# Linear attention on one core: scores from a block-diagonal q, or head by head in row groups of 32

## What is computed

```python
xn = layernorm(x)                       # 2048 x 512
q, k, v, u = split(xn @ W_qkvu.T, 4);  q, k = silu(q), silu(k)      # 16 heads of 32
# for each block of tokens and each head, with a state kv (32 x 32):
o = (q * q_decay) @ kv + ((q @ k.T) * diag_decay) @ v
kv = block_decay * kv + (k * k_decay).T @ v
branch1 = (u * (o * rsqrt(mean(o * o) + eps))) @ W_out.T
idx = sort(top_k(xn @ w_router, 256));  branch2 = xn, with attention and MLP on xn[idx]
out = x + branch1 + branch2
```

## Time and profile before

| | us |
|---|---|
| median of 3 runs | 670.95 |
| lowest, highest run | 670.15, 677.82 |
| span of the profiled execution (first to last instruction) | 664.6 |
| median less span | 6.3 |
| TensorE matmuls busy in the span | 563.0 (85%) |
| VectorE, ScalarE, GpSimd busy | 406.3 (61%), 332.8 (50%), 256.9 (39%) |

### The profile page before, as it was taken

The page is one execution under the profiler, slowest core; times in us unless marked ns, Lnnn a source line. Parts: engine busy times, 40 slices in busy tenths (PEclk is TensorE's granted clock), DMA queues, the critical chain, the costliest instruction groups (busy, mean ns, idle before and its releaser), DMA issues.

```text
span 664.6 us, 10529 instructions
## 1 busy us (share of the span) xinstructions
PE 563.0 (85%) x3946; PEld 496.2 (75%) x3946; DVE 406.3 (61%) x777; ACT 332.8 (50%) x574; POOL 256.9 (39%) x149
## 2 busy tenths in 40 slices
PE   2897999999999999999989665594678768789993
PEld 2787888898898888988868554484577757589992
DVE  5648546644655555555677877687988996513231
ACT  4786544454463455544778780234545544545430
POOL 3435334223332332332221443545430522247771
PEclk9897999999999999999998987796789897989998
DMA  9300012101001110001000414232311123115432
GB/s 289 138 18 31 2 33 33 33 2 33 33 2 33 34 33 0 18 17 50 30 17 1 143 34 125 99 103 87 126 64 64 64 72 119 65 64 175 154 117 32
DMA packets 24067, 42.93 MB, mean 65 GB/s; under 512 B 4112, under 2 KB 4112, under 8 KB 23888
## 3 DMA queue, kind: packets, MB, share of 16 engines
q1 hardware_dynamic: 23472, 40.93, 19.0%
q0 software_dynamic: 544, 1.31, 1.1%
...
## 4 chain that ended last, share of the span: by engine, by line
PE 58%; issue 13%; DVE 13%; ACT 9%; POOL 3%; DMA 2%; SPq 1%; ACTq 0%; DVEq 0%; POOLq 0%
PE bank L1116 17%; PE bank L1072 9%; PE bank L1074 8%; PE bank L1073 8%; PE bank L1109 6%; PE bank L1161 3%; ACT marks L398 2%; DVE rope L849 2%; PE bank L1198 2%; DVE staged L852 2%; DMA XX<-in_x 2%; PE bank L1220 2%; DVE rope L847 2%; PE bank L1142 1%; ACT whi L420 1%
## 5 line engine op out<-in xcount | busy, mean ns | idle before, releaser
L1022 POOL TENSOR_TENSOR wlo<-raw,whi 128x2048 fp32r<-128x2048 f32 x24 | 112.0, 4668 | 121.1 <-ACT whi L420 121.1
L1116 PE MATMUL bank<-xTh,Wh 128*128 128x256 f32 x384 | 120.1, 313 | 8.2 <-DVE Wl L630 4.9
L1116 PE MATMUL bank<-xTl,Wh 128*128 128x256 f32 x384 | 110.3, 287 | 0.0
L1116 PE MATMUL bank<-xTh,Wl 128*128 128x256 f32 x384 | 110.2, 287 | 0.0
L1116 PEld LDWEIGHTS bank<-xTh,Wh 128*128 128x128 f32 x384 | 75.2, 196 | 20.4 <-issue 16.7
L683 DVE TENSOR_TENSOR QBl<-QT,QBh 32x256 fp32r<-32x256 f32 x128 | 73.9, 577 | 13.7 <-ACT QBh L391 12.4
L1072 PE MATMUL bank<-HTh,whi 128*128 128x256 f32 x224 | 66.5, 297 | 14.4 <-DVE staged L840 9.7
L1116 PEld LDWEIGHTS bank<-xTl,Wh 128*128 128x128 f32 x384 | 75.3, 196 | 0.2
L1116 PEld LDWEIGHTS bank<-xTh,Wl 128*128 128x128 f32 x384 | 75.0, 195 | 0.0
L1073 PE MATMUL bank<-HTl,whi 128*128 128x256 f32 x224 | 66.4, 296 | 0.0
L1074 PE MATMUL bank<-HTh,wlo 128*128 128x256 f32 x224 | 66.2, 296 | 0.0
...
## 6 DMA issues: line engine op xcount, KB each, us to landing
...
```

Source lines behind the costliest of these rows:

```text
L1022: Q.tensor_tensor(wlo[b % 3][:], raw[b % 2][:], whi[b % 3][:].bitcast(f32), ALU.subtract)\
L1116: ins = T.matmul(bank[:, half * GROUP:(half + 1) * GROUP], w[:, k, cols], xt[:, g % 2, k, :], start=m % steps == 0, stop=m % steps == step ...
```

## The change

The block-diagonal operand goes. q is kept as it is, in `qh` and `ql` (rows, 4 tiles, 128 tokens), each written by one instruction of 512 elements per partition. `score(N)` does all 16 heads at once: for each tile j and each of the three products, four matmuls, one a head, each contracting only its 32 rows (a row group of the array) over 128 columns, and each into a bank of its own (0, 1, 6, 7). `by_row` puts `A` and `DEC` into the order of the banks. The attention output, the sum of squares and the output projection now share bank 4; turned keys, transposes and keys-by-values share bank 5; the ranking's small products use bank 2. The order within a chunk becomes: score, tile 0, rms(N-1), keys turned, tile 1, output projection (N-1), transposes, tile 2, `attend` (state part, then all 16 heads in a row), new keys-by-values, tile 3. On VectorE the mask comes first in a chunk, and the state product last. On GpSimd `q_decayed(N)` stands in slot N rather than in the slot before it. Two memsets of the old operand fall away.

```diff
-        QBh, QBl = (sb(n, [P, 2, 4, P], f32r, ca) for n in ("QBh", "QBl"))
+        qh, ql = (sb(n, [P, NK, P], f32r, ca) for n in ("qh", "ql"))
...
         B = [ctx.enter_context(nc.psum_tensor(f"bank{i}", [P, 512], f32)) for i in range(8)]
 
-        def score_bank(N, half, b):
-
-            return B[2 + b] if half and N >= N_TILES - CH else B[b]
+        score_banks = [B[0], B[1], B[6], B[7]]
+        out_bank, turn_bank, pick_bank = B[4], B[5], B[2]
+
+        def by_row(h):
+
+            return NK * (h % 4) + h // 4
 
...
-            def q_high(N, half):
-
-                act.wait_ge(proj_sb, NPROJ * (N // CH) + 4), act.wait_ge(bm_ok, 1)
-                act.wait_ge(s_ps, 2 * N + half), act.wait_ge(q_lo, 2 * N + half)
+            def q_high(N):
+
+                act.wait_ge(proj_sb, NPROJ * (N // CH) + 4)
+                act.wait_ge(s_ps, N), act.wait_ge(q_lo, N)
                 cols = slice(N % CH * P, (N % CH + 1) * P)
-                for r in range(4):
-                    rows = slice(DH * r, DH * r + DH)
-                    ins = S.activation(QBh[rows, :, r, :], QT[rows, N // CH % 2, 2 * half:2 * half + 2, cols], ACT.Copy)
-                ins.then_inc(q_hi, 1)
+                S.activation(qh[:], QT[:, N // CH % 2, :, cols], ACT.Copy).then_inc(q_hi, 1)
...
-            def q_low(N, half):
-                dve.wait_ge(q_hi, 2 * N + half + 1), dve.wait_ge(s_ps, 2 * N + half)
+            def q_low(N):
+                dve.wait_ge(q_hi, N + 1), dve.wait_ge(s_ps, N)
                 cols = slice(N % CH * P, (N % CH + 1) * P)
+                V.tensor_tensor(ql[:], QT[:, N // CH % 2, :, cols], qh[:].bitcast(f32), ALU.subtract).then_inc(q_lo, 1)
+
+            def mask(N):
+
+                dve.wait_ge(s_ps, N + 1), dve.wait_ge(pv_ps, N), dve.wait_ge(dec_ok, 1)
                 for r in range(4):
-                    rows = slice(DH * r, DH * r + DH)
-                    ins = V.tensor_tensor(QBl[rows, :, r, :], QT[rows, N // CH % 2, 2 * half:2 * half + 2, cols],
-                                          QBh[rows, :, r, :].bitcast(f32), ALU.subtract)
-                ins.then_inc(q_lo, 1)
-
-            def mask(N, half):
-
-                dve.wait_ge(s_ps, 2 * N + half + 1), dve.wait_ge(pv_ps, N), dve.wait_ge(dec_ok, 1)
-                for b in range(2):
-                    heads = slice(8 * half + 4 * b, 8 * half + 4 * b + 4)
-                    V.tensor_tensor(A[:, heads, :], tiles4(score_bank(N, half, b)[:]), DEC[:, heads, :], ALU.mult)\
+                    heads = slice(NK * r, NK * r + NK)
+                    V.tensor_tensor(A[:, heads, :], tiles4(score_banks[r][:]), DEC[:, heads, :], ALU.mult)\
                         .then_inc(masked, 1)
...
-            V.memset(QBh[:].bitcast(f32), 0.0)
-            V.memset(QBl[:].bitcast(f32), 0.0)
             V.memset(state[:], 0.0).then_inc(bm_ok, 1)
             dve.wait_ge(bm_ok, 1)
             for N in slots_of_chunks:
                 M = N + LN_AHEAD
+                if N >= 0:
+                    mask(N)
                 if M < N_TILES:
...
                 if N == N_TILES - 1:
-                    q_low(N, 1)
                     place_tokens()
-                if N >= 0:
-                    mask(N, 0)
                 if 0 <= N < N_TILES - 1:
                     dve.wait_ge(kt_ps, N + 1), dve.wait_ge(kv_ps, N)
-                    V.tensor_tensor(kdec[:], B[5][:], KD[:], ALU.mult).then_inc(k_dec, 1)
-                if 0 <= N < N_TILES - 1:
-                    q_low(N, 1)
-                if N == -1:
-                    q_low(0, 0)
+                    V.tensor_tensor(kdec[:], turn_bank[:], KD[:], ALU.mult).then_inc(k_dec, 1)
+                if -1 <= N < N_TILES - 1:
+                    q_low(N + 1)
...
-                if N >= 0:
-                    mask(N, 1)
-                    if N == N_TILES - 2:
-                        choose_tokens()
-                    if N >= 1:
-                        final(N - 1)
-                    if N < N_TILES - 1:
-                        q_low(N + 1, 0)
-                        state_part(N)
+                if N == N_TILES - 2:
+                    choose_tokens()
+                if N >= 1:
+                    final(N - 1)
...
-                    V.tensor_tensor(uo[:], tiles4(B[4][:]), UT[:, N // CH % 2, :, at], ALU.mult).then_inc(uo_ok, 1)
+                    V.tensor_tensor(uo[:], tiles4(out_bank[:]), UT[:, N // CH % 2, :, at], ALU.mult).then_inc(uo_ok, 1)
+                if 0 <= N < N_TILES - 1:
+                    state_part(N)
...
-                pool.wait_ge(state_ok, N), pool.wait_ge(bm_ok, 1)
+                pool.wait_ge(state_ok, N), pool.wait_ge(bm_ok, 1), pool.wait_ge(decays_ok, 1)
...
-                if N >= 0 and N < N_TILES - 1:
-                    q_decayed(N + 1)
+                if N >= 0:
+                    q_decayed(N)
                 if -1 <= N < N_TILES - 1:
                     k_low(N + 1)
-                if N == -1:
-                    q_decayed(0)
...
-            def score(N, half):
-
-                pe.wait_ge(k_hi, N + 1), pe.wait_ge(q_hi, 2 * N + half + 1)
-                pe.wait_ge(k_lo, N + 1), pe.wait_ge(q_lo, 2 * N + half + 1)
-                if half and N >= N_TILES - CH:
-                    pe.wait_ge(masked, 4 * N), pe.wait_ge(proj_sb, NPROJ * G)
-                else:
-                    pe.wait_ge(masked, 4 * N + 2 * half)
-                for b in range(2):
-                    j = 2 * half + b
-                    ins = split_matmuls(score_bank(N, half, b)[:], (kh[:, j, :], kl[:, j, :]),
-                                        [q[:, b].rearrange("p r m -> p (r m)") for q in (QBh, QBl)], True, True)
+
+            def score(N):
+
+                pe.wait_ge(k_hi, N + 1), pe.wait_ge(q_hi, N + 1)
+                pe.wait_ge(k_lo, N + 1), pe.wait_ge(q_lo, N + 1)
+                pe.wait_ge(masked, 4 * N)
+                for j in range(NK):
+                    for n, (k, q) in enumerate(((kh, qh), (kh, ql), (kl, qh))):
+                        for r in range(4):
+                            rows = slice(DH * r, DH * r + DH)
+                            ins = T.matmul(score_banks[r][:, j * P:(j + 1) * P], k[rows, j, :], q[rows, j, :],
+                                           start=n == 0, stop=n == 2)
                 ins.then_inc(s_ps, 1)
 
...
+            def rms(N):
+
+                pe.wait_ge(sq_ok, N + 1), pe.wait_ge(consts, 1)
+                for k in range(NK):
+                    ins = T.matmul(out_bank[:, 0:1], sq[:, k, :], ones1, start=k == 0, stop=k == NK - 1)
+                ins.then_inc(rms_ps, 1)
...
+            def keys_turned(N):
+
+                pe.wait_ge(xt_lo, min(N + XT_AHEAD, N_TILES)), pe.wait_ge(kv_masked, N)
+                for k in range(NK):
+                    ins = T.transpose(turn_bank[:, k * P:(k + 1) * P], KT[:, N // CH % 2, k, N % CH * P:(N % CH + 1) * P],
+                                      ident[:])
+                ins.then_inc(kt_ps, 1)
+
+            def attend(N):
+
+                pe.wait_ge(q_dec, N + 1), pe.wait_ge(state_ok, N), pe.wait_ge(bm_ok, 1), pe.wait_ge(final_ok, N)
+                for j in range(NK):
+                    ins = T.matmul(out_bank[:, j * P:(j + 1) * P], state[:, j, :], qdec[:, j, :], start=j == 0,
+                                   stop=False, skip_group_check=True)
+                ins.then_inc(inter_ps, 1)
+                pe.wait_ge(proj_sb, NPROJ * (N // CH) + 6), pe.wait_ge(masked, 4 * N + 4)
+                for h in range(NH):
+                    j, r = h // 4, h % 4
+                    ins = T.matmul(out_bank[DH * r:DH * r + DH, j * P:(j + 1) * P],
+                                   VT[:, N // CH % 2, N % CH, DH * h:DH * h + DH], A[:, by_row(h), :], start=False,
+                                   stop=True, skip_group_check=True)
+                ins.then_inc(pv_ps, 1)
+
+            def new_keys_values(N):
+
+                pe.wait_ge(k_dec, N + 1), pe.wait_ge(xt_lo, min(N + XT_AHEAD + 1, N_TILES))
+                for j in range(NK):
+                    cols = slice(j * P, (j + 1) * P)
+                    ins = T.matmul(turn_bank[:, cols], kdec[:, cols], VT[:, N // CH % 2, N % CH, cols], start=True,
+                                   stop=True)
+                ins.then_inc(kv_ps, 1)
 
...
-                buf = N // CH % 2
-                score(N, 0)
-                if N == 0:
+                score(N)
+                if tiles:
                     project(tiles[0])
-                elif tiles:
-                    project(tiles[0], lambda step: rms(N - 1, step))
-                else:
-                    for step in range(3 * NK):
-                        rms(N - 1, step)
+                    rms(N - 1)
                 if N < N_TILES - 1:
...
-                pe.wait_ge(uo_ok, N), pe.wait_ge(sq_ok, N)
-                for j in range(NK):
```

(31 more changed lines are left out.)

85 lines of the change are left out of this document (24 added, 61 removed).

## The result

The changed kernel takes 651.7 us (649.7 to 655.0, 4 runs) against 673.4 (670.2 to 677.8, 4 runs) for the kernel before: a ratio of 0.969, 95% interval 0.964 to 0.975. A second set gave 644.8 (643.2 to 645.9) against 671.2, ratio 0.963 (0.958 to 0.968). It is faster, as forecast, but the first result lies outside the range of 619 to 650, and the gain is 21.7 us (26.4 in the second set) where 38.2 was forecast.

The account below looks back on a forecast made before the run. TensorE alone was taken to set the pace in chunks 1 to 11. Gains of 6.7 + 24.2 + 6.3 + 1 = 38.2 us off a 664.6 span gave 626.4; with 6.3 for the median, 632, range 619 to 650.

Parts of the forecast that it names:

- the steady part: Chunks 1 to 11: TensorE alone sets the pace; scores gain 1.2, heads 1.0, so 22.76 us a chunk becomes 20.55.
- rival 1: Scores: loads of different row groups queue up, 0.11 us each, 4.0 more a chunk; 696 us, slower; chance 0.08.
- rival 2: Scores: a round cannot hide its loads behind the same row group's matmuls, 0.17 us a round; 643 us; chance 0.12.
- rival 3: Scores: rounds at the cheap end, 0.06 us each, 0.6 less a chunk; 622 us; chance 0.06.
- rival 5: Scores: two groups overlap, not four; 24 steps of 0.11 us, 1.3 more a chunk; 653 us; chance 0.06.
- The turning point: Scores: the price at which the whole change turns; a load-and-matmul pair may cost 0.078 us.
- the start: Up to chunk 1: two memsets gone, 2.06 us; chunk 1 begins at 63.3 instead of 70.0, gain 6.7.
- The median of the runs lies 6.3 above the span: Last step of the sum: 6.3 us added to the span of 626.4 gives 632.7, say 632.
- eleven steady chunks: Chunks 1 to 11 on TensorE: 2.2 us saved in each, 24.2 us in all.
- What follows the indices is not changed and waits for them; I take it as it is: Stretch after the indices: taken at its length before, 254.9 us, no gain.
- chunks 12 to the indices: Chunks 12 and 13 take 46 us, gain 6.3; chunk 14 to the indices 36 against 37.1, gain 1.
- Rival 4: Ranking: steady part as forecast, but `final` and the root behind comparisons and counts take back 7.3; 639 us; chance 0.08.

Follow-up runs that it names:

- e2_heads_together: Kernel before with only its 16 heads A by VT in one stretch after the third projection tile, scores as before; ratio 0.987 to the kernel before.
- first profile: Profiled execution of the changed kernel that came with the first result; span 653.2 us.
- second profile of before: The kernel before run once more, unchanged, on another occasion; span 668.4 us, median 671.8.
- second profile: The changed kernel run once more, unchanged, on another occasion; span 641.5 us, ratio 0.963 to the kernel before.
- e3_row_by_row: Changed kernel with the same 48 score matmuls a chunk ordered one row group after the other instead of four side by side; 713.0 us.
- e5_blocks_later: Changed kernel with GpSimd's low parts of weight blocks 0 and 1 moved behind the gather and behind the normed rows; 641.3 us, ratio 0.959 to the kernel before.
- e6_root_first: Changed kernel with ScalarE's square root for chunk N-1 ahead of its counting of marks instead of behind it; ratio 0.963 to the kernel before.
- e11_counts_later: Changed kernel, chunks 12 to 14 reordered: next chunk's high parts before ScalarE's first two counts, chunk N-1's last addition before VectorE's second two comparisons; 631.8 us, ratio 0.937.

## Why the prediction was wrong

**Right: the steady part, where nothing disturbs it.** Chunks 20.5 us apart (20.37 and 20.63 in turn) where 20.55 was forecast, without a wait in them. The heads' gain was 0.98 for 1.0 by e2_heads_together; the rest 1.28 for 1.2. The single rows differ a little and cancel: scores 1.49, not 1.65, heads 1.01, not 1.2, while `sq`, which I put at no change, seems to have been partly hidden before (not tested by itself). Rivals 1, 2, 3 and 5 fall: a round costs 0.11, four groups run side by side. The turning point against rival 1 (0.078 a pair) was right in kind too: row by row a pair costs 0.09 and the kernel is slower than before, 713.0 against 670.0, part of it by the clock.

**Wrong in the first profile, right by luck in the second: the start.** The memsets were sized rightly: from the second profile of before to that of the changed kernel the scores of chunk 0 came 2.0 us sooner, for 2.06. But chunk 1 at 63.3, exact in the second profile, is two errors that cancel: scores began at 43.55, not 42.15, and chunk 0 took 19.75, not 21.15, since TensorE waited 0.89 us for `kdec`, not 3.3, and the clock stayed up. In the other profiles with this start and an early product (but for e3_row_by_row) chunk 1 began at 62.4 to 65.1, with the wait at 2.8. For the first profile the forecast was 6.0 us too early. The step that failed there is the sum "The start", which has the two memsets and no term for what stands ahead of them. In before's profile the third product had begun 0.58 us ahead of GpSimd's subtraction; I read its 0.69 us and not how near the other stood.

**Wrong: "The median of the runs lies 6.3 above the span".** In all runs the time is 1.8 above the span. Before's profiled execution took 664.6 + 1.8 = 666.4 us, less than each of the four runs of before in the first set (670.2 to 677.8). The difference was between executions: the forecast started from a quick execution of before. Added to the new span, the 6.3 stood for nothing; it was 4.5 too much and hid as much of what the other steps lacked. The median lies 19.0 above the forecast, the span that answers to it (651.7 − 1.8) 23.5.

**Wrong: eleven steady chunks.** The gaps in 7 and 11 and the clock behind them cost 6.0 us in the first profile, 3.0 in the second (231.3 and 228.4 against the 225.4 without gaps); as the steady chunks were 0.7 better in all than forecast, 5.2 and 2.3 of that show as error. The sum had no term for how fast TensorE uses up its instructions; 96 of them in 1.5 us, right behind a slow fetch, is what the change added.

**Wrong: "What follows the indices is not changed and waits for them; I take it as it is".** It took 8.7 to 9.9 us longer than in the profile that I had, 6.6 to 7.7 longer than in the second one of before: part of it is that quick execution again. From 3.7 to 5.3 of these lie before the first unit: the norm takes 5.4 to 5.8 us, where the two profiles of before have 2.2 and 3.7, since the new timing puts it wholly under GpSimd's subtraction (e5_blocks_later won back 3.6), and `uo(15)` comes behind a projection that the new order has put behind the indices' products. The other 2.5 to 5.0, from the first unit to the end, aren't explained: 235.3 and 236.2 in the two profiles of before, 237.7 in e2_heads_together, 238.7 and 240.2 after.

**Roughly right, for part of the reason: chunks 12 to the indices.** 47.1 and 48.7 for 46, 39.1 and 39.2 for 36. I named the root behind the counts as the wait, and it was; but e6_root_first shows that it only covered another, `final` behind `ql` behind the counts, which e11_counts_later removed. From chunk 14 to the indices the step that failed is chunk 14 itself, for which my layout had comparisons reached "about 2 us sooner" and no wait for the root or for `final`. It took 24.4 us where the profiles of before have 19.6 and 20.4: TensorE waited 6.7 us for the root and 4.0 for `final`, and was granted 0.65 of its clock over the chunk, against 0.91 and 0.75. The stretch from chunk 15 to the indices got shorter, 14.75 against 17.4 and 18.2. "GpSimd's first weight block in front of the one-hot marks" did cost 4 there, but it was no new cost. In VectorE's timeline of before the same subtraction, from 396.47 to 401.15, holds up the pieces of `QBl`, four of which take 2.3 us by the earlier trace rows:

```profile
396.15 6.15 DVE L683 TENSOR_TENSOR QBl<-QT,QBh 32x256 fp32r<-32x256 f32 x4 [2.75 <-ACT QBh L391]
```

Rival 4 (nothing won in the ranking) was the nearest to the truth in its mechanism, 52.3 + 37.05 = 89.35 having become 86.2 to 87.9, 1.5 to 3.2 won of 7.3; that its 639, like rival 2's 643 and rival 5's 653, lies nearer to the result than the forecast is chance.

By the second profile the errors of the five stages are 0, 2.3, 1.1, 3.1 and 8.7, but for rounding the 15.1 us between 626.4 and 641.5. By the first, whose set gave the result, they are 6.0, 5.2, 2.7, 3.2 and 9.9, 26.8 between 626.4 and 653.2.
